# A three-stage kernel in one block: stages 1, 2 and 3 follow each other engine by engine

## The reference

```python
xn = layernorm(x)                                   # eps 1e-5, no scale or shift
# attention: 16 heads of 16, positions up to 64 apart
q, k, v = split(xn @ Wqkv + bqkv)
scores = where(|i - j| <= 64, q k^T * 16**-0.5, min)
attn = (softmax(scores) v) @ Wout + bout
# experts: 8 of 256 -> 1024 -> 256, the two best for each token
logits = xn @ router_w + router_b
gating = softmax(logits of the top 2)
ffn = sum_e gating_e * (relu(xn @ w1_e + b1_e) @ w2_e + b2_e)
out = x + attn + ffn
```

## Time and profile before

| | us |
|---|---|
| median of 3 timed runs | 956.04 (954.45 to 956.12) |
| profiled execution, device time | 957.17 |
| its span, first to last instruction | 955.1 |
| TensorE busy | 903.1 |
| VectorE busy | 824.7 |
| ScalarE busy | 740.7 |
| GpSimd busy | 480.5 |
| stage 1, to TensorE's last product | 98.0 |
| stage 2, to TensorE's last product | 494.3 |
| stage 3, to the end | 955.1 |

### The profile page before, as it was taken

The page is one execution under the profiler, slowest core; times in us unless marked ns, Lnnn a source line. Parts: engine busy times, 40 slices in busy tenths (PEclk is TensorE's granted clock), DMA queues, the critical chain, the costliest instruction groups (busy, mean ns, idle before and its releaser), DMA issues. The chain is left out here.

```text
span 955.1 us, 27555 instructions
## 1 busy us (share of the span) xinstructions
PE 903.1 (95%) x7684; PEld 876.4 (92%) x7684; DVE 824.7 (86%) x2171; ACT 740.7 (78%) x1985; POOL 480.5 (50%) x700
## 2 busy tenths in 40 slices
PE   4989799899999999999969999999999999999996
PEld 3878788889999999999969999999999999999996
DVE  5876699998888888888857999999999999999995
ACT  3545699899999999999956777777777776777773
POOL 5120013236465646555544666556666666556663
PEclk9999799999999999999998999999999999999999
...
GB/s 143 322 268 308 169 79 75 117 122 136 136 136 135 137 135 133 136 141 148 105 87 163 37 34 44 46 36 36 34 34 43 47 49 49 35 44 35 36 22 1
DMA packets 69867, 95.33 MB, mean 100 GB/s; under 512 B 15549, under 2 KB 48960, under 8 KB 69696
## 3 DMA queue, kind: packets, MB, share of 16 engines
...
q0 software_dynamic: 17024, 16.88, 11.2%
...
## 5 line engine op out<-in xcount | busy, mean ns | idle before, releaser
L1029 ACT ACTIVATE weights_qkv<-weights_qkv,low 128x256 f32<-128x256 f32 (+1 forms) x512 | 240.2, 480 | 1.1 <-DVE low L832 1.1
L1456 ACT ACTIVATE hid<-ps_experts,b_s 128x256 f32<-128x256 f32 x312 | 131.0, 473 | 117.5 <-PE ps_experts L1523 87.4
L1344 POOL DMA_INDIRECT out<-y,target x78 | 137.3, 1761 | 127.4 <-DVE y L1422 113.8
L843 DVE TENSOR_TENSOR pt<-ps_attend,pt 128x512 fp32r<-128x512 f32 (+1 forms) x256 | 158.4, 620 | 39.9 <-ACT pt L1042 39.3
L1123 PE MATMUL ps_attend<-pt,v_m 128*80 128x256 f32 (+7 forms) x1536 | 187.8, 271 | 2.3 <-DVE inv_t L856 1.8
L1539 PE MATMUL ps_experts<-w_hi,h_hi 128*128 128x256 f32 x624 | 175.4, 281 | 1.1 <-DVE h_lo L1391 1.1
L1523 PE MATMUL ps_experts<-xgt_hi,w_hi 128*128 128x256 f32 x624 | 173.7, 278 | 2.8 <-DVE xgt_lo L1382 2.8
L1123 PEld LDWEIGHTS ps_attend<-pt,v_m 128*80 128x80 f32 (+3 forms) x1536 | 171.4, 162 | 4.2 <-issue 4.2
L1523 PE MATMUL ps_experts<-xgt_hi,w_lo 128*128 128x256 f32 x624 | 173.6, 278 | 0.0
L1523 PE MATMUL ps_experts<-xgt_lo,w_hi 128*128 128x256 f32 x624 | 173.5, 278 | 0.0
L1539 PE MATMUL ps_experts<-w_lo,h_hi 128*128 128x256 f32 x624 | 172.6, 277 | 0.0
...
## 6 DMA issues: line engine op xcount, KB each, us to landing
...
qk_hi<-weights_qkv SPq DMA_DIRECT2D x16, 512.0 KB, 4.8
qk_lo<-weights_qkv SPq DMA_DIRECT2D x16, 512.0 KB, 5.5
q_st<-qk_hi SPq DMA_DIRECT2D x128, 64.0 KB
k_st<-qk_hi SPq DMA_DIRECT2D x128, 64.0 KB
weights_qkv<-in_x SPq DMA_DIRECT2D x8, 512.0 KB, 4.3
xn_rows<-weights_qkv SPq DMA_DIRECT2D x8, 512.0 KB, 5.2
...
```

The source lines that it names most:

```text
L843: v.tensor_tensor(lo[:, f:l], ps[:, bank_t[h], 0:l - f], hi[:, f:l].bitcast(F32), ALU.subtract).then_inc(s_plo, 1)
L1029: ins = act.activation(wt[:, ring, at_tile(i)], wt[:, ring, at_tile(i)], ACT.Exp, bias=low[:, ring, i:i + 1], scale=-1.0, accum_out=total[ ...
L1344: pool.indirect_dma_start(out_tokens, bass.IndirectOffsetOnAxis(ap=target[:, h:h + 1], axis=0), y[:, h], None, bounds_check=T - 1, oob_is_ ...
L1456: ins = act.activation(hid[:, n % 2, j], ps[:, bank_h[n], j * ROWS:(j + 1) * ROWS], ACT.Relu, bias=b1[:, ds(e * FC + 2 * n + j, 1)])
```

## The change

All three stages stand in one block, `g.block`. The engines no longer meet between stages; where an engine needs something of an earlier stage it waits for that stage's semaphore (`g.projection[...]`). All later semaphores are created at the start (`LATER`) and raised by GpSimd. To make room at the same time, stages share tiles: `work` and `split` are the token halves in stage 1, the transposed weights and output halves in stage 2, and hidden values and rows in stage 3, and the experts' split weights lie in `q_st`, `v_m` and `k_st`.

At the start the first tokens come in two loads, and batch 0 is normalised half by ScalarE and half by VectorE; GpSimd's clears wait for VectorE's half. ScalarE splits the q weights first, then the tokens, then the rest of the weights; TensorE asks for the q weights alone before its first projection. In every batch TensorE waits for each half of each chunk by itself at m = 0, and uses the low weights second and the low tokens third.

At the end of stage 2 GpSimd gathers the first rows within the last batch, after its 15th head. ScalarE and VectorE split the first expert's weights around the last output, TensorE transposes the first rows between the halves of the last projection, and the gathers of the second and third rows follow at once. What stage 3 did of this before its first step (the rows' transposes, three weight halves on either engine) is gone from it.

```diff
-                load(0, 0)
+                for half, landed in ((0, s_xfirst), (1, s_x)):
+                    t = slice(half * TB // 2, (half + 1) * TB // 2)
+                    sp.dma_start(x[:, 0, t], x_rows[0, :, t]).then_inc(landed, 16)
...
+                sp.wait_ge(s_xnfirst, 1 + START)
...
-                pool.wait_ge(s_rstd, 1 + START)
+                start(pool, g.later.values())
+                start(pool, g.s_out)
+                pool.wait_ge(s_xnfirst, 1 + START)
...
-                statistics(0, 0)
+                v.wait_ge(s_ident, 2 + START)
+                v.tensor_copy(g.ident_r[:], g.ident[:])
+                statistics(0, 0, True)
                 inverse_root(0, True)
+                v.wait_ge(s_rstd, 1 + START)
+                for t in range(TB // 2, TB):
+                    ins = v.tensor_scalar(xn[:, 0, t, :], x[:, 0, t, :], rstd[:, t:t + 1], shift[:, t:t + 1],
+                                          ALU.mult, ALU.add)
+                ins.then_inc(s_xnfirst, 1)
                 v.wait_ge(s_whi, 1 + START)
                 v.scalar_tensor_tensor(out=w_lo[:, :, 0:D], in0=w_raw[:, :, 0:D], scalar=SCALE,
                                        in1=w_hi[:, :, 0:D].bitcast(F32), op0=ALU.mult, op1=ALU.subtract
                                        ).then_inc(s_wlo, 1)
+                lo_of_tokens(0, 0)
                 v.wait_ge(s_whi, 2 + START)
                 v.tensor_tensor(w_lo[:, :, D:3 * D], w_raw[:, :, D:3 * D], w_hi[:, :, D:3 * D].bitcast(F32),
                                 ALU.subtract).then_inc(s_wlo, 1)
                 v.wait_ge(s_whi, 3 + START)
                 v.tensor_tensor(w_hi[:, :, 3 * D + E:WIDE], rw_raw[:], w_hi[:, :, 3 * D:3 * D + E].bitcast(F32),
                                 ALU.subtract).then_inc(s_wlo, 1)
-                lo_of_tokens(0, 0)
                 statistics(1, 1)
...
-                    for t in range(TB):
+                    for t in range(TB // 2):
                         ins = act.activation(xn[:, 0, t, :], x[:, 0, t, :], ACT.Identity,
                                              bias=shift[:, t:t + 1], scale=rstd[:, t:t + 1])
                     ins.then_inc(s_xn, 1)
 
                 variance_root(0)
+                norm_first()
                 act.wait_ge(s_wqkv, 16 + START)
                 act.activation(w_hi[:, :, 0:D], w_raw[:, :, 0:D], ACT.Copy, scale=SCALE).then_inc(s_whi, 1)
+                hi_of_tokens(0, 0)
...
                 act.activation(w_hi[:, :, D:3 * D], w_raw[:, :, D:3 * D], ACT.Copy).then_inc(s_whi, 1)
-                norm_first()
                 act.wait_ge(s_w, 48 + START)
                 act.activation(b_s[:, 0:DC], b_qk[:, 0:DC], ACT.Copy, scale=SCALE).then_inc(s_bq, 1)
                 act.activation(b_s[:, DC:2 * DC], b_qk[:, DC:2 * DC], ACT.Copy).then_inc(s_bq, 1)
                 act.activation(w_hi[:, :, 3 * D:3 * D + E], rw_raw[:], ACT.Copy).then_inc(s_whi, 1)
-                hi_of_tokens(0, 0)
                 variance_root(1)
...
+                pe.wait_ge(s_xnfirst, 1 + START)
                 transpose_tokens(0, 0)
-                pe.wait_ge(s_wlo, 3 + START)
+                pe.wait_ge(s_wlo, 1 + START)
...
-                    pe.wait_ge(s_lo, 2 * b + 2 + START)
-                    pe.sem_inc(g.tick, 1)
                     for m in range(2 * DC):
                         pe.wait_ge(s_qklo, 4 * b + m - 1 + QK0)
+                        if m == 0:
+                            pe.sem_inc(g.tick, 1)
                         n = 0
                         for c in range(DC):
-                            for w, xx in ((w_hi, hi), (w_hi, lo), (w_lo, hi)):
+                            for w, xx in ((w_hi, hi), (w_lo, hi), (w_hi, lo)):
+                                if m == 0 and w is w_hi:
+                                    if xx is hi:
+                                        pe.wait_ge(s_hi, 2 * b + c + 1 + START)
+                                    else:
+                                        pe.wait_ge(s_lo, 2 * b + c + 1 + START)
+                                    pe.sem_inc(g.tick, 1)
                                 ins = pe.matmul(ps[:, bank_qk[m % 2], :], w[:, c, m * P:(m + 1) * P],
                                                 xx[:, c, :], start=(n == 0), stop=(n == 5))
                                 n += 1
                         ins.then_inc(s_qk, 1)
                         if m == 1:
+                            pe.wait_ge(s_wlo, 3 + START)
...
+        bank_last = (bank_m, bank_t[1])
...
-        with nc.Block() as block:
+        with nullcontext(g.block) as block:
...
+                def gather_first():
+                    pool.wait_ge(s_rows, 16 + START)
+                    pool.tensor_copy(g.index[:, 0], g.rows[:, 0:2, 0].bitcast(U32)).then_inc(s_idx, 1)
+                    pool.wait_ge(s_idx, 1 + START)
+                    for h in range(2):
+                        pool.indirect_dma_start(
+                            g.first_rows[:, h].bitcast(F32), None, g.xn_dram,
+                            bass.IndirectOffsetOnAxis(ap=g.index[:, 0, h:h + 1], axis=0),
+                            bounds_check=T - 1, oob_is_err=False).then_inc(g.s_g[h], 16)
...
+                        if last and n == 14:
+                            gather_first()
+
+                pool.wait_ge(g.projection["s_vlo"], 2 * B + START)
                 batch(0, True, False)
                 batch(1, False, False)
+                pool.wait_ge(g.projection["s_table"], 16 + START)
                 with pool.Fori(2, B - 1) as b:
                     batch(b, False, False)
                 batch(B - 1, False, True)
-                pool.wait_ge(s_rows, 16 + START)
-                pool.tensor_copy(g.first_index[:], g.rows[:, 0:2, 0].bitcast(U32)).then_inc(s_first, 1)
...
+                v.wait_ge(g.projection["s_const"], 5 + START)
+                v.wait_ge(g.projection["s_xnout"], 16 * B + START)
...
+                v.wait_ge(s_named, 1 + START)
+                first = v.value_load(g.step_expert[0:1, 0:1], min_val=0, max_val=E - 1)
+
+                def lo_of_w1(n):
+                    cols = slice(n * F // 2, (n + 1) * F // 2)
+                    v.wait_ge(s_w1hi, n + 1 + START)
+                    v.tensor_tensor(g.w1_lo[:, :, cols], g.w1_of(first)[:, :, cols], g.w1_hi[:, :, cols].bitcast(F32),
+                                    ALU.subtract).then_inc(s_w1lo, 1)
+
+                lo_of_w1(0)
...
-                add_projected(B - 1, 0, bank_t[0])
-                add_projected(B - 1, 1, bank_t[1])
+                v.wait_ge(s_xhi, 1 + START)
+                v.tensor_tensor(g.xt_lo.rearrange("p c n -> p (c n)"), ps[:, bank_t[0], :],
+                                g.xt_hi.rearrange("p c n -> p (c n)").bitcast(F32), ALU.subtract).then_inc(s_xlo, 1)
+                for h in range(2):
+                    add_projected(B - 1, h, bank_last[h])
+                lo_of_w1(1)
+                half = slice(0, FC // 2)
+                v.wait_ge(s_w2hi, 1 + START)
+                v.tensor_tensor(g.w2_lo[:, half], g.w2_of(first)[:, half], g.w2_hi[:, half].bitcast(F32),
+                                ALU.subtract).then_inc(s_w2lo, 1)
...
+                act.wait_ge(s_named, 1 + START)
+                first = act.value_load(g.step_expert[0:1, 0:1], min_val=0, max_val=E - 1)
+
+                def hi_of_w1(n):
+                    cols = slice(n * F // 2, (n + 1) * F // 2)
+                    act.activation(g.w1_hi[:, :, cols], g.w1_of(first)[:, :, cols], ACT.Copy).then_inc(s_w1hi, 1)
+
+                act.wait_ge(s_wlast, 16 + START)
+                hi_of_w1(0)
                 inverse_out(2 * B - 1, False)
+                hi_of_w1(1)
                 act.wait_ge(s_proj, 2 * (B - 1) + START)
                 for h in range(2):
                     act.wait_ge(s_enda, h + 1 + START)
                     act.activation(a_hi[:, 1, half_of(h)], inv_t[:, half_of(h)], ACT.Copy).then_inc(s_endhi, 1)
+                act.wait_ge(s_tr4, 1 + START)
+                act.activation(g.xt_hi.rearrange("p c n -> p (c n)"), ps[:, bank_t[0], :], ACT.Copy
+                               ).then_inc(s_xhi, 1)
+                act.wait_ge(s_wload, 32 * (E - 1) + START)
+                half = slice(0, FC // 2)
+                act.activation(g.w2_hi[:, half], g.w2_of(first)[:, half], ACT.Copy).then_inc(s_w2hi, 1)
+                act.wait_ge(s_b1, 16 + START)
...
+                pe.wait_ge(g.projection["s_qklo"], 4 * B + START + 1)
                 scores(0, 1, True)
                 scores(0, 2)
+                pe.wait_ge(g.projection["s_lgout"], B + START)
...
+                for h in range(2):
+                    project(B - 1, h, range(0, 6), bank_last[h])
+                for h in range(2):
+                    pe.wait_ge(g.s_g[h], 16)
                 for c in range(DC):
                     for h in range(2):
-                        project(B - 1, h, range(6 * c, 6 * c + 6), bank_t[h])
```

(33 more changed lines are left out.)

280 lines of the change are left out of this document (131 added, 149 removed).

## The result

The changed kernel takes 959.55 us (median of five runs, 958.15 to 960.14) where the kernel before takes 955.79 (five runs beside them): a ratio of 1.0040, with a 95% interval of 1.0025 to 1.0054. It is slower, by 0.4%. The forecast was 937.8 us, in a range that ended at 945.5, with a chance of 0.02 for a slower kernel. Two things happened at once. The gains ahead of stage 3 came: in the profiled executions the experts' first matmul starts 17.75 us earlier (485.24 instead of 502.99), where the prediction's terms, without what it expected of the first layer, make 15.9. And stage 3 gave back more than that. Its granted clock rose earlier in stage 1 and was low for a shorter time in stage 2.

What follows compares the result with a forecast made beforehand. TensorE, busy 903.1 of 955.1 us, was taken as the bound, with idle or low-clock time at four places. Terms 2.0 + 4.8 + 2.5 + 9.1 = 18.4 off the 956.04 median gave 937.6, taken as 937.8; range 933.5 to 945.5.

Steps and rivals of the forecast that it cites:

- rival (d): Stage 3: expert matmuls slow down with weights in other tiles; 0.24 us a layer cancels the gain, 0.30 gives 961; chance 0.02.
- 1 start: Start of stage 1: halved token loads and shared normalising bring the second eviction and later work forward; 2.0 us.
- 2 loop: Loop of stage 1: TensorE's six waits for low tokens at a batch's start all go; 4.8 us.
- 3 stage 1 to 2: Between stages 1 and 2: engines no longer meet, so the first mask starts earlier; 2.5 us.
- 4 stage 2 to 3: Between stages 2 and 3: experts start 6.6 us earlier and the first layer gains 2.5 at full clock; 9.1 us.
- what is gained is the second eviction: Start of stage 1: VectorE's second eviction follows the first at once, at 19.1 instead of 20.79; 1.6 us.
- Rival (a): End of stage 1: transfers set the pace, losing 3.0 of 4.8 and 1.5 of 2.5 us; 942.3 us, chance 0.17.
- Rival (b): Start of stage 2: the clock stays up behind shorter gaps, gaining 2.4 us more; 935.4 us, chance 0.13.
- Rival (c): Start of stage 3: low clock or a jump costs time, losing 3.6 of 9.1 us; 941.4 us, chance 0.17.

Runs made afterwards that it cites:

- b_pad: The kernel before with 64 bytes of padding ahead of w1_hi and 192 ahead of b1_s, so all its tiles start at byte 0; 976.74 us.
- a_best: The changed kernel with paddings alone: experts' weights at byte 192 of 256, rows, hidden activations and ident_r at byte 0; 938.01 us, ratio 0.9808.
- a_start: a_best with the start undone: first tokens in one transfer, normalised by ScalarE alone, weights' split awaited whole; 937.27 us, ratio 0.9811.
- a_idle: The changed kernel with one wait ahead of TensorE's first expert layer, until the last expert's weights have landed; 979.11 us.
- a_joint: a_best with tiles at other bytes: streamed rows and second-layer weights at 0, loaded first-layer weights and hidden activations at 64; 935.65 us, ratio 0.9788.
- a_best2: The same kernel as a_best, measured once more on another occasion; 937.42 us, ratio 0.9804.

## Why the prediction was wrong

**Step that failed: the pace of the expert matmuls, which the sum puts at nothing, and with it rival (d), dismissed at 0.02.** The sum has no term for how long the other 77 layers take, since "the edit leaves that code as it is". The runs show 0.31 us more in each first layer and 0.29 in each second, some 22 us in all, and that the tiles' start bytes cause it: b_pad brings it into the kernel before, and a_best takes it out of the changed one. Of the two prices that rival (d) names, one, 0.30 us a layer and 961 us, came out almost to the number (959.55); the prediction takes it from no row, so that the number is luck. The only argument against the rival was that "stage 3 already reads from several tiles at one pace". That argument looked at which tiles are read and not at their start bytes: in the kernel before, every loaded tile differs from the streamed one of its matmul, 192 and 0, so that one pace says nothing about equal bytes. The evidence for a slower pace was in the trace before too: where they follow each other without a wait, most 128x256 products with v in stage 2 have 116 to 120 ns between their starts, those of stage 3 have 113.3, and 118 in the part of the first expert layer that ran at the full clock (the last 20 of its 48). A form that takes two times in one kernel is a warning when an edit moves its operands.

**Sum: right, for a kernel in which the matmuls keep their pace.** Forecast 18.4 us; a_best gained 18.3 and 17.8 (956.32 less 938.01, 955.25 less 937.42). That it fits so closely is in part luck: the start brought some 1.5 us less than forecast, and the boundary and the end of stage 2 somewhat more. Term by term:

| step | forecast | measured |
|---|---|---|
| 1 start | 2.0 | 0.5 (with the loop edit in), 1.0 (without); uncertain by 2 |
| 2 loop | 4.8 | 4.9, uncertain by 2 |
| 3 stage 1 to 2 | 2.5 | 4.0, uncertain by 2 |
| 4 stage 2 to 3 | 9.1 | 9.6 in the traces; 6.2 of it for the boundary |

1. The mechanism at the start was read rightly: first projection at 11.10 (forecast 11.2), a wait before the third (2.46, forecast 1.7). The gain was mis-sized: the batch ends as early with the old start. The step that failed is "what is gained is the second eviction", 1.6 us from 20.79 to 19.1. The 20.79 is the late clock's: VectorE's second eviction there waits for a product that TensorE made at the low clock, and in b_pad, with the same code, it stands at 19.64. In the change it follows at 18.8, in a_start as well, since the first eviction is just as early there (18.09 and 18.00). a_start's third projection starts at 18.80, behind a wait of 0.31 us, the changed kernel's at 18.89, behind one of 2.46: TensorE starts earlier only to wait longer.
2. No waits are left in the loop and the transposes follow at 21.12, 30.64, 40.36, 49.77, 59.27, 68.79 and 78.29: a cycle of 9.5, forecast 9.6. Rival (a) fell: the transfers, with a share of 0.85 and 311 GB/s in the loop, did not set the pace.
3. The first mask comes 2.1 us after the end of TensorE's last product of stage 1 (90.71), forecast 1.7, before 4.2. Its place, 92.79, is the one that the terms give (99.7 less 6.8). Undoing the boundary costs 4.0 us, and the 1.5 more than forecast lie within the uncertainty. Rival (b) fell in the changed kernel's profiled execution: the clock went to 0.50 by 98 us (the windows above), behind gaps of 2.45 and 0.78 us on TensorE. But this is no property of the kernel. a_idle has the same code up to the experts and the same two gaps (2.45 and 0.78), and its clock stayed up there; it was low for 3.4 us only at 168:

```profile
98.00:102.00 4.00, 2.97 (x24) 2.57 (x24) 3.68 (x17) 3.81 (x16) 0.44 (x2) 1.00 0.99 203
```

a_joint's stayed up through all of stage 2, and from the first scores to the last it takes 377.3 us, a_best2 379.6: the 2.3 us are what rival (b) was priced at (2.4). The Trainium skill (TensorE: Matmul & The Clock Gate, HAM oscillation — how this bites in real kernels) lets only long gaps between matmuls throttle the clock; these two traces, throttled and not behind the same short gaps, show that the length of the gaps alone doesn't decide it.
4. TensorE waits 1.37 us for the spreading of the last inverses (forecast 1 to 2), and the first layer takes 6.02 us at the full clock (forecast 5.5 to 6). Rival (c) fell. From the start of the last of stage 2's last scores to the second layer of the first expert step are 21.85 us (469.53 to 491.38), before 31.46 (480.17 to 511.63): 9.6 us, forecast 9.1. From the start of the last product of stage 2 to the experts are 0.38 instead of 8.94 us.
